# In the widest tile's step: probabilities copied ahead of the swap, low halves made ahead of the maximum, transposes done ahead of the side work

## The reference

```
x = x + 0.5 * ffn(layernorm(x))      # top-2 of 8 LoRA experts over a shared gated MLP of 704
x = x + attention(layernorm(x))      # 16 heads of 128, causal, rotary embedding
x = x + 0.5 * ffn(layernorm(x))

# attention
q, k, v = x @ wq, x @ wk, x @ wv
q, k    = rope(q) / sqrt(128), rope(k)
probs   = softmax(where(causal, q @ k.T, -1e30))
out     = (probs @ v) @ wo, summed over heads
```

## Time and profile before

| | |
|---|---|
| median of 3 runs | 1498.7 us (1498.55 to 1500.48) |
| profiled execution, its own time | 1501.39 us |
| its span, first to last instruction | 1499.6 us |
| mean granted TensorE clock | 0.985 |
| busy: TensorE, VectorE, ScalarE, GpSimd | 1420.6, 1058.1, 906.9, 786.6 us |
| attention, 311.4 to 1143.4 us of the span: TensorE busy | 816.94 of 832.00 us |

### The profile page before, as it was taken

How to read it: one execution, slowest core, us unless ns; L and a number is a source line. 1 busy time by engine, 2 the same in 40 slices (tenths; PEclk the granted TensorE clock), 3 DMA queues, 4 the chain that set the end, 5 groups by cost and what they waited for, 6 DMA issues and landing times.

```text
span 1499.6 us, 25599 instructions
## 1 busy us (share of the span) xinstructions
PE 1420.6 (95%) x8912; PEld 1265.2 (84%) x8912; DVE 1058.1 (71%) x2368; ACT 906.9 (60%) x1881; POOL 786.6 (52%) x701
## 2 busy tenths in 40 slices
PE   5899999699999999999999999999999987899998
PEld 4688888588999899999989998999899975788886
DVE  7567776877767776777677777776776776575665
ACT  3534443577767767777677667776776653444433
POOL 4555444355555555565555555555555543655443
PEclk9899999899999999999999999999999999999999
DMA  4000001000000000000000000000000030000000
GB/s 165 1 1 1 1 1 50 22 8 16 8 8 8 15 8 8 15 8 8 15 1 8 23 1 8 22 1 8 8 1 2 1 110 1 0 15 1 15 15 15
DMA packets 11422, 23.40 MB, mean 16 GB/s; under 512 B 928, under 2 KB 5024, under 8 KB 11168
## 3 DMA queue, kind: packets, MB, share of 16 engines
q1 hardware_dynamic: 11296, 21.78, 4.4%
HBM read 19.68 MB, written 2.10 MB: 15 GB/s over the span
## 4 chain that ended last, share of the span: by engine, by line
PE 84%; DVE 11%; issue 3%; ACT 1%; POOL 1%; DMA 0%; DVEq 0%; ACTq 0%; POOLq 0%
PE ps L1278 24%; PE ps L1280 24%; PE ps L1279 24%; PE ps L1619 9%; DVE ps L1217 2%; DVE pT_l L314 1%; DVE mixed L1020 1%; DVE hid L1010 1%; PE ps L1291 1%; DVE stats L870 1%; DVE hid L997 0%; DVE spread L889 0%; POOL um_l L314 0%; DVE xn L889 0%; DVE part_sum L1036 0%
## 5 line engine op out<-in xcount | busy, mean ns | idle before, releaser
L597 POOL TENSOR_SCALAR probs<-probs,inv_sum 128x128 f32<-128x128 f32 (+7 forms) x256 | 213.2, 833 | 383.0 <-DVE inv_sum L1173 382.9
L1217 DVE CUSTOM_DVE_ANT_0 ps<-ps,causal 128x128 f32<-128x128 f32 (+7 forms) x256 | 195.0, 762 | 210.9 <-PE ps L1280 209.2
L825 ACT ACTIVATE probs<-ps,neg_max 128x128 f32<-128x128 f32 (+7 forms) x256 | 189.1, 739 | 79.3 <-DVE neg_max L1217 79.3
L314 POOL TENSOR_TENSOR hid_l<-hid,hid_h 128x512 fp32r<-128x512 f32 x80 | 107.5, 1344 | 182.8 <-ACT hid_h L680 182.8
L314 DVE TENSOR_TENSOR pT_l<-ps,pT_h 128x512 fp32r<-128x512 f32 (+3 forms) x384 | 200.7, 550 | 2.3 <-ACT pT_h L804 1.9
L804 ACT ACTIVATE pT_h<-ps 128x512 fp32r<-128x512 f32 (+3 forms) x384 | 174.3, 490 | 37.2 <-PE ps L1619 34.7
L586 POOL TENSOR_TENSOR rot_sin<-swapped,rope 128x512 f32<-128x512 f32 x128 | 165.4, 1293 | 54.7 <-ACT swapped L781 54.7
L1619 PE MATMUL ps<-ident,probs 128*128 128x128 f32 x1152 | 170.6, 275 | 21.7 <-DVE pT_l L314 19.3
L1280 PE MATMUL ps<-pT_h,v_l 128*128 128x256 f32 (+1 forms) x640 | 179.2, 280 | 0.0
L1279 PE MATMUL ps<-pT_l,v_h 128*128 128x256 f32 (+1 forms) x640 | 179.1, 280 | 0.0
L1278 PE MATMUL ps<-pT_h,v_h 128*128 128x256 f32 (+1 forms) x640 | 178.2, 278 | 0.8 <-DVE oA_l L314 0.8
(11 more groups left out here) (184 smaller groups left out, 4068.4 us busy)
## 6 DMA issues: line engine op xcount, KB each, us to landing
w_raw<-attn_w SPq DMA_DIRECT2D x32, 256.0 KB, 2.7
w_in<-ffn_w SPq DMA_DIRECT2D x12, 576.0 KB, 8.6
x_sb<-x_in SPq DMA_DIRECT2D x4, 512.0 KB, 5.5
out<-x_sb SPq DMA_DIRECT2D x3, 512.0 KB, 2.9
rope<-rope_w SPq DMA_DIRECT2D x1, 1024.0 KB, 7.9
w_in<-ffn_w SPq DMA_DIRECT2D x2, 264.0 KB, 4.9
expand_raw<-expand_w SPq DMA_DIRECT2D x2, 256.0 KB, 7.8
out<-x_sb SPq DMA_DIRECT2D x2, 256.0 KB, 2.1
```

The source lines that it names most:

```text
L314: return eng.tensor_tensor(dst, src, high.bitcast(F32), ALU.subtract)
L597: pool.tensor_scalar(probs[s % 4][:, 0:n], probs[s % 4][:, 0:n], inv_sum[:, s % 4:s % 4 + 1], 1.0, ALU.mult, ALU.mult).then_inc(probs_read ...
L825: act.activation(probs[t % 4][:, 0:a * n].rearrange("p (a n) -> p a n", a=a), view, ACT.Exp, bias=neg_max[:, t % 4:t % 4 + 1], scale=-1.0, ...
L1217: dve.tensor_tensor_reduce(out=view, in0=view, in1=causal[:, SEQ - a * n:].rearrange("p (a n) -> p a n", a=a), scale=-SCALE, scalar=HUGE, ...
```

## The change

A helper names the step before which things are moved: `widest_next(t)` is true for i = 6, so `widest_next(t - 1)` for i = 7.

- ScalarE: the swap of the projection made in step i = 6 is no longer issued at the end of that step but in step i = 7, behind the copies of the transposed probabilities.
- VectorE: in step i = 7 the low halves of the transposed probabilities (of tile i = 4) are made ahead of the row maximum instead of behind it.
- TensorE: in step i = 7 the transposes (of tile i = 5) are done right behind the scores, ahead of the values or the output projection.

Nothing else moves, and no instruction is added or removed.

```diff
+        def widest_next(t):
+            return t % SEQ_TILES == SEQ_TILES - 2
...
@@ ScalarE, attention: behind the copies of pT_h
+                    if 0 < t < STEPS and widest_next(t - 1):
+                        before = side_work(p, t - 1, first, last)
+                        if before:
+                            swap_halves(before[2], misc_bank(t - 1))
...
@@ ScalarE, attention: behind the exponential
-                    if side and side[0] == "proj":
+                    if side and side[0] == "proj" and not widest_next(t):
                         swap_halves(side[2], misc_bank(t))
...
@@ VectorE: the loop over tile_groups becomes a function turned_low(q, s)
+                    tile = tile_of_step(p, t, T_LAG + 1, first)
+                    widest = t < STEPS and widest_next(t - 1)
+                    if tile and widest:
+                        turned_low(*tile)
                     if t < STEPS:
                         view, a, n = score_view(t % 2, t % SEQ_TILES)
...
-                    if tile:
...
+                    if tile and not widest:
+                        turned_low(*tile)
...
@@ TensorE, attention
+                    widest = t < STEPS and widest_next(t - 1)
+                    tile = tile_of_step(p, t, T_LAG, first)
...
                         if t < STEPS:
                             scores(p, t, first)
+                        if tile and widest:
+                            turn(*tile)
                         side(p, t, first, last)
...
-                    tile = tile_of_step(p, t, T_LAG, first)
-                    if tile:
+                    if tile and not widest:
                         turn(*tile)
```

More of the change, by code:

```diff
@@ L1196, in norm_early, with turned_low @@
                     layer_norm_low(n, c, LN_BANKS[c])
+            def turned_low(q, s):
+                i = s % SEQ_TILES
+                half = P * (i % 2)
+                for n, (slot, count) in enumerate(tile_groups(i)):
+                    dve.wait_ge(pT_high, groups_before(q, s) + n + 1)
+                    bank = T_BANK + (GROUPS_AT[i] + n) % 2
+                    low(dve, pT_l[i // 2 % 2][:, slot:slot + count, half:half + P],
+                        ps[:, bank, 0:P * count].rearrange("p (a b) -> p a b", a=count),
+                        pT_h[i // 2 % 2][:, slot:slot + count, half:half + P]).then_inc(pT_ready, 1)
             def attention(p, first, last):
@@ L1227, in attention @@
                         layer_norm_low(2 * CHUNKS - 1, CHUNKS - 1)
-                    tile = tile_of_step(p, t, T_LAG + 1, first)
-                    if tile:
[L1230 to L1238, removed]
+                    if tile and not widest:
+                        turned_low(*tile)
                     side = side_work(p, t, first, last)
```

## The result

The changed kernel takes 1504.8 us (median of 9 runs, 1502.6 to 1506.7) against 1499.9 us of the kernel before in the same rounds (9 runs, 1497.9 to 1503.5): ratio 1.003, interval 1.0021 to 1.004. It is slower by 0.3%; forecast were 1501.7 us and a ratio of 1.002. The profiled execution of it took 1504.8 us (span 1503.0), 3.4 more than the one before; forecast for it were 1504.4. The medians differ by 4.9 us (the interval is 3 to 6), the two traces by 3.4, and the forecast was 3.0.

The account below looks back on a forecast made before the run. TensorE, busy 95% of the span, was taken as the bound, its waits for pT_l as the loss. Value steps +10.6, output steps -7.3 and the end -0.3 gave +3.0 us: 1501.7 us, range 1491 to 1511.

Parts of the forecast that it names:

- main step: In value steps the wait ahead of tile 5 shrinks but returns at tiles 6 and 7; pT_l waits below 8 us refute.
- wait at tile 7: Transposes of tile 7 after a value step: a new wait for pT_l near 0.9 us.
- value step: The 16 widest-score steps where TensorE makes values after the scores: +0.66 us each, +10.6 us in all.
- the sum's overlap with GpSimd's normalisation: VectorE's rotation sum in value steps, 0.11 longer for overlapping GpSimd's normalisation of tile 6: claimed to go.
- hold at tile 6: Transposes of tile 6 after a value step: a new wait of 0.27 us for their low halves.
- output step: The 15 widest-score steps where TensorE makes an output projection: 0.49 us gained each, -7.3 us in all.
- last step: The very last widest step, with neither values nor output: 0.3 us gained of its 2.1 us wait.
- Rival C: GpSimd wins the port in output steps, holding the rotation's sum: 1508.5 us in half, 1515.2 in all; chance 0.28.
- Rival A: No wait comes back later: value steps give 0.39, output steps about 0.67; -16.6 us, 1482.1 us; chance 0.12.
- Rival B: Transposes of tile 5 start with no hold in value steps: -3.9 us, 1494.8 us; chance 0.15.

Follow-up runs that it names:

- e2: The change only in the 16 steps where TensorE makes values after the widest scores, against the kernel before: 1509.8 us, ratio 1.0072.
- e3: Changed kernel with both halves of v from the widest step made one step later, against the kernel before: 1489.3 us, ratio 0.9929.
- e6: Changed kernel with GpSimd's normalisation of tile 6 ahead of its low half of qk in output steps, against the kernel before: 1520.0 us, ratio 1.0122.
- e8: Changed kernel, both halves of v one step later, next step's swap also behind the copies of tile 6; against the kernel before: 1482.5 us, ratio 0.9876.
- e1: The change only in output steps and the very last step, value steps in the old order, against the kernel before: 1494.3 us, ratio 0.9966.
- e7: Changed kernel, v's halves one step later, output's sum into x behind the low halves of tile 5; against the kernel before: 1496.7 us, ratio 0.997.
- e5: The kernel before with only v's two halves of the widest step made one step later, without the change: 1500.2 us, ratio 0.9993.

## Why the prediction was right

**The main step held: a wait moved, it was not removed.** The wait at tile 7 appeared with 0.76 in the list; counted as the prediction counts, from the start that the last product ahead of it would allow (646.33 + 0.12) to 647.37, it is 0.92 (forecast near 0.9). The value step lost 0.64 where 0.66 was forecast. e2 shows that loss alone, e3 takes its cause away and the loss with it. All waits for pT_l together are 17.9 us, far from the 8 that would have refuted the step.

**Inside that step two terms were off and cancelled.** The copies of tile 4 stood 0.89 ahead of the last score product (636.79 and 637.68), where 0.77 was carried over from before; so v_h was 0.66 later, not 0.79. And the sum's overlap with GpSimd's normalisation did not go: it takes 0.78 (642.12), as it had 0.79. The normalisation stands behind the swap on its way through GpSimd's queue, and the swap was moved by as much as v_h: both ends of the overlap moved together (641.35 to 642.12 is 0.77, as 638.78 to 639.55). The prediction counted the move for one of them. That the two errors, 0.13 and 0.11 to 0.12, took each other away is luck. (A slip beside them: 637.06 + 1.73 is 638.79, not 638.77.)

**The hold at tile 6 was there, in another place.** Forecast were 0.27 at its transposes. Measured: no wait is listed there, but TensorE stood ahead of the products of probabilities and v, which could follow the last projection product (641.85) after 0.23, at 642.08, and came at 642.35, 0.27 late. VectorE read the bank for oB_l until 642.20 (641.79 + 0.41), and the code has the products wait for that (`weigh`, `o_ready`); no row names the wait in this step, so that it was this one is inferred.

**The output step was right in sign and a quarter too large:** 0.39 instead of 0.49. The output started 0.66 behind the transposes, not 0.60 (the swap left its bank at 668.99, but in value steps the values start 0.08 behind the swap's end and here the output 0.14, so what cost the 0.06 is not shown); the sum into x started 2.78 behind the last score product (forecast 2.73, before 2.82); the rotation's sum took 0.71, not 0.68. The copies of tile 6 came 7.10 behind the last score product instead of 7.31 before: 0.21 earlier, where 0.31 was forecast. Term by term the sum came out as +10.3 for the value steps (forecast 10.6), -5.8 for the output steps (-7.3), -0.5 for the last step (-0.3) and -0.6 behind the attention (nothing): +3.4 for +3.0. So the total is closer than its terms, and that is luck too. The clearest miss is the output step, 1.5 us of 7.3.

**Rival C** (GpSimd wins the port) was the dangerous one, and did not occur, for a reason that the prediction missed. It had both start at once, with a swap 0.65 behind the copies. The swap came 0.78 to 0.79 behind them (636.79 to 637.57, 667.00 to 667.79), right behind the end of both copies (636.79 + 0.76 is 637.55), and GpSimd's normalisation came later with it: 671.59, 0.14 behind the sum. e6 shows such a loss, with a longer instruction of GpSimd's. **Rival A** (no wait comes back, -16.6 us) is not what this order does; only e8 gains as much (-18.3), and by another sum, 0.63 in each kind of step where the rival had 0.39 and 0.67. **Rival B** needed the transposes of tile 5 unheld; they were held by 0.33 (637.92 to 638.25).

## What to carry to other kernels

Follow a removed wait to the next semaphore behind it on each in-order queue: here TensorE's loss of 0.85 us at one place fell to 0.33, and a wait of 0.76 came up at another because the values' copy, now later, held ScalarE's exponential behind it and VectorE's low half of v. A reordering is only worth what its followers allow, so move the consumers that became late with it (e3: from +0.3% to -0.7%), and test the kinds of step apart, since a total near zero can be two effects of opposite sign (e1, e2). If two engines contend, compute both starts with the same move applied to both.

## What the runs showed of the hardware

**Two starts 0.15 apart.** A VectorE sum of two SBUF operands (128x512) takes 0.68 undisturbed, and took 0.71 in the changed kernel where it had started 0.14 ahead of GpSimd (671.45). Where GpSimd's low half of qk (about 1.29) was 0.12 to 0.17 ahead, all 118 such sums of the ten traces took 1.68 to 1.73: 1.0 us for one lost start. Semaphores can set this up: a sum that had to wait for GpSimd's previous instruction started 0.15 behind GpSimd's next one, in e3 (631.18 and 631.33) and in e7 (666.33 and 666.48). The Trainium skill has the rule that the first to issue holds the port pair to its end ("SBUF — State Buffer", "Who interferes with whom"). By that rule, the traces, which give starts and not issues, agree for starts 0.14 apart, and differ for the 0.05 of rows 7, where the second won.

**Starts closer than 0.1.** That the second wins is no rule either. In the trace of before, 12 of the 15 sums that started 0.04 to 0.06 behind GpSimd's normalisation of 128 columns took 0.68, and three, as the one at 586.54, took 0.85 to 0.87 while GpSimd kept its 0.36 to 0.38. In the trace of the changed kernel all 29 that started 0.04 to 0.09 behind took 0.82 to 0.87. So an order that depends on such starts can't be forecast from one pair of rows, as the prediction did.

**A late end that was not the order.** The last spacing of e5 is 24.12 (1207.01 to 1231.13), against 22.89 before. TensorE waited 2.13 for pT_l shortly ahead of it in both traces, but in e5 the granted clock was 0.50 from 1226.0 to 1229.0 (the lower level, 1.2 GHz), with products 0.21 apart instead of 0.12; before, it was 1.00 from 1227.3 to 1231.0. So these 1.2 us belong to the clock in that one execution and not to e5's order. Why it fell in the one and not in the other is open.
